# Layer 0's opening: first product without the identity, loads reordered, band patterns stored in the order read, first band read unguarded

## The chip, the core and the metric

The kernel runs on one core of a Trainium2 chip. A core has five engines that run their own instruction streams: PE (matrix products and transposes, with weight loads as a stream of their own), DVE and ACT (elementwise work and reductions), POOL (elementwise, slower) and SP, which here only issues DMAs. ACT also issues some. DMAs run on 16 DMA engines; an engine issues one and goes on, and whoever needs the data waits on a semaphore. The metric is the device time of one execution in microseconds, the median of several.

## What is computed

A four-layer network on tensors of 8 x 512 tokens x 128 channels. The change lies at the start of layer 0, an attention with 16 heads of 8 channels and relative positions in logarithmic buckets (DeBERTa's form). Before it the tokens are normalised (NT = 32 tiles of 128 tokens). Cut to what matters:

```python
q = split_heads(hidden_states @ Wq + bq)
k = split_heads(hidden_states @ Wk + bk)
v = split_heads(hidden_states @ Wv + bv)
scores = jnp.einsum('bhqd,bhkd->bhqk', q, k) / scale
rel = build_relative_position(S, S, BUCKETS, MAX_REL)
pos_k = (rel_embeddings @ Wk + bk).reshape(2 * ATT_SPAN, nH, d)
c2p_att = jnp.einsum('bhqd,hpd->bhqp', q, pos_k)
c2p = jnp.take_along_axis(c2p_att, c2p_pos, axis=-1)
p2c_att = jnp.einsum('bhkd,hpd->bhkp', k, pos_k)
p2c = jnp.swapaxes(jnp.take_along_axis(p2c_att, p2c_pos, axis=-1), -1, -2)
scores = scores + (c2p + p2c) / scale
probs = jax.nn.softmax(scores, axis=-1)
```

## The kernel before

Every engine has its own function per layer (`l0_pe`, `l0_dv`, `l0_ac`, `l0_po`, `l0_sp`); the order of the work on an engine is the order in which that function writes it, and semaphores join them. `Engine.wait_ge` leaves out a wait already seen.

**Setup.** `run_sp` and `run_ac` issue the first loads: `relT`, `oh`, `pat` (SP) and `wk`, `bkt` (ACT) count on `ld_pos`, five times 16 = 80; `X[:, 0:8]` (512 KB) on `ld_end`, the rest of x (1536 KB) on `ld_x`, the identity on `ld_id`, the other small ones on `ld[0]`. PE multiplies `relT` by `wk` (the position keys), DVE adds `bkt` (`posk`), PE multiplies `posk` by `oh`: these are the band patterns PGF. DVE and ACT split PGF into three 16-bit parts, `PGS` (128 x 3 x 256). SP writes PGS to DRAM (`pgd`) and reads it back in another layout into `PGO`, whose 16 matrices of 128 x 128 for each of two sides hold, for one head each, 8 rows at the places that `PLACES` lists. Meanwhile DVE normalises the tokens in four groups of 8 tiles (`norm_stats`, `root`, `tokens`) into `XN`, PE transposes them, four tiles at a time (eight times, `n_tr`), and ACT copies them to `XT` (`n_xt`). `root(c)` on DVE waits for a square root by ACT (`norm_root`), which stands behind patterns and copies in ACT's order.

**Split q and k.** PE makes q and k of the first sequence, ACT and DVE split them in 16-bit parts (`split_ac`, `split`). SP writes these parts to DRAM (`q_write(0, 0)`, `q_write(0, 1)`: three DMAs each, `q_write(0, 2)`: one) and loads them again by groups of four heads (`load_group`, `load_upper`).

**Bands.** For head n, `g_of(n, 0)` and `g_of(n, 1)` on PE multiply these by `PGO`, DVE's `g_out` adds a step that POOL made (`corr`) and puts the sums into `GG[n % 2]`, which must have been cleared once. SP writes GG to DRAM (`write(n)`) and reads it back one element shorter per row (`read(n)`), which shifts each row by its number, into `CD[n % 3]`. CD[0] lies in the arena AR; CD[1] and CD[2] lie in XN's memory, and so may only be written once all XN tiles have been transposed: `read` waits for `n_tr` 8. POOL masks a band (`own_band`), PE adds its transpose to the scores, DVE adds the masked own part (`add`), takes the maximum (`most`), ACT exponentiates.

**Loop.** 128 heads x 4 steps (`STEPS0` = 512 + 28). In each step PE does at most one small product of the next sequence, one `g_of`, the transposes of an earlier step, and the scores. `G_AT`, `CORR_AT`, `WRITE_AT` and `READ_AT` say at which step what is issued.

Of the kernel before, what the change touches and what calls it, by code (L numbers as in the profile page):

```python
# [12 lines left out]
NB, NT, NH = 8, 32, 16  # L13
# [129 lines left out]
def flat(ap):  # L143
    return ap.rearrange("p a b -> p (a b)")
# [83 lines left out]
def program(nc, a, out):  # L228
    ctx = ExitStack()
    with ctx:  # L230
# [6 lines left out]
        X = sb("X", [128, NT, 128])  # L237
# [180 lines left out]

        PT_0, XN_0, GG_0 = 1, 2, 5
        PGO_0, VA_0, HALF_0 = 1, 3, 4  # L420
        sgn, set_mm, set_dv, set_ac, sel_ok, pg_w, pg_r = (sem("set_" + k) for k in ("sgn", "mm", "dv", "ac", "sel", "pgw", "pgr"))
# [55 lines left out]
        def l0_pe(pe):  # L477
            pe.wait_ge(ld_id, 16)
            pe.wait_ge(ld_pos, 80)
# [109 lines left out]
            def pv(G, jb):  # L589
# [10 lines left out]
                if jb == 3:  # L600
                    ins.then_inc(pv_mm, 1)

            pe.wait_ge(dv_init, XN_0)
            for j in range(4):
# [12 lines left out]
            pe.wait_ge(*emptied[number["g0", 0, 0]])  # L617
            pe.wait_ge(pg_r, 12 * 16)
            pe.wait_ge(dv_init, GG_0)
            for n in range(2):  # L620
# [22 lines left out]
        def l0_dv(dv):  # L643
# [68 lines left out]
            tokens(12, 16).then_inc(n_xd, 1)  # L712
            for k in range(2):
                dv.e.memset(GG[k], 0.0).then_inc(dv_init, 1)
            norm_stats(dv, 0, NT0, 2, False)
# [11 lines left out]
            def g_out(n, x):  # L727

                dv.wait_ge(g_mm, 2 * n + x + 1)
                dv.wait_ge(p_cr, 2 * n + x + 1)  # L730
                dv.wait_ge(dv_init, GG_0)
                if n >= 2:
# [215 lines left out]
        def l0_po(po):  # L948
            po.e.memset(PGO, 0.0).then_inc(po_init, 1)
            for k in range(2):  # L950
                po.e.memset(VA[k], 1.0).then_inc(po_init, 1)
            po.e.memset(minus_half, -0.5).then_inc(po_init, 1)
# [68 lines left out]
        def l0_sp(sp):  # L1021
            sp.wait_ge(set_dv, 6)
            sp.wait_ge(set_ac, 2)
            sp.e.dma_start(pgd, PGS).then_inc(pg_w, 16)
            sp.wait_ge(pg_w, 16)
            sp.wait_ge(po_init, PGO_0)
            for k in range(2):
                for part, first, step, times in PLACES[1 - k]:
                    for x in range(first, first + step * times, step):
                        src = bass.AP(pgd.tensor, part * 256 + k * 128, [[16 * 768, 8], [768, 16], [1, 128]])  # L1030
                        sp.e.dma_start(PGO[8 * x:8 * x + 8, k], src).then_inc(pg_r, 16)

# [49 lines left out]
            def read(n):  # L1082

                sp.wait_ge(wr[n % 2], 16 * (n // 2 + 1))
                sp.wait_ge(n_tr, 8)
                if n >= 3:
                    sp.wait_ge(s_mm, 4 * (n - 2))
                    sp.wait_ge(p_w, 2 * (n - 2))
                src = bass.AP(scr.tensor, n % SLOTS * 128 * ROW + 64, [[ROW - 1, 128], [1, BACK]])
                sp.e.dma_start(CD[n % 3], src).then_inc(rd[n % 3], 16)  # L1090
# [1660 lines left out]
        def run_ac(g):  # L2751
# [3 lines left out]
            ac.e.dma_start(X[:, 0:8, :], a["x"][:, 0:8, :]).then_inc(ld_end, 16)  # L2755
            ac.e.dma_start(X[:, 8:NT, :], a["x"][:, 8:NT, :]).then_inc(ld_x, 16)
            ac.e.dma_start(wo, a["l0_wo"]).then_inc(ld[0], 16)
# [31 lines left out]
        def run_sp(g):  # L2789
            sp = Engine(g, own["sp"])  # L2790
            for dst, name in ((relT, "relT"), (oh, "oh"), (pat, "pat")):
                sp.e.dma_start(dst, a[name]).then_inc(ld_pos, 16)
            sp.e.dma_start(ident192[:, :], a["ident"]).then_inc(ld_id, 16)
            for dst, name in ((wq, "l0_wq"), (colb, "l0_cols"), (mask16, "mask16"), (wv, "l0_wv"), (bvt, "l0_bvt"),
                              (steps, "steps"), (window, "window"), (sw, "l0_sw")):
                sp.e.dma_start(dst, a[name]).then_inc(ld[0], 16)
            l0_sp(sp)
            after_l0(sp)
# [85 lines left out]
```

## Time and profile before

| | |
|---|---|
| Median of 3 executions | 2166.33 us (2162.15 to 2167.49) |
| The profiled execution | 2157.39 us, span 2155.6 us |
| Mean granted clock of PE | 0.966 of full speed |
| Busy: PE, DVE, ACT, POOL | 89%, 79%, 67%, 56% of the span |
| DMA | 264.01 MB, 122 GB/s in the mean, 263 to 312 GB/s in slices 2 to 16 of 40 |

The profile is one execution. The span runs from its first to its last instruction; 1.8 us lie around it. A row of the timeline gives the start and length of an instruction, or of several merged ones (xN), and in brackets how long the engine had been idle before it and what ended that. Layer 0 takes about the first 890 us of the span.

### The profile page before, as it was taken

Reading aid. Unit: us, or ns where it says so; the run is one execution under the profiler, and the core shown is the slowest. Engines: PE = TensorE matmul, PEld = TensorE weight load, DVE = VectorE, ACT = ScalarE, POOL = GpSimd, SP = SyncE. Lnnn points to the kernel's source line nnn. Section 1 sums busy time; section 2 is a strip of 40 time slices with the busy share of each in tenths; the row PEclk is TensorE's granted clock in tenths of the full one; section 3 lists DMA queues with packets and bytes.
Section 4 is the critical chain, followed back from the end, with each engine's and each line's share of the span. In section 5 each row is a group of like instructions: output and inputs, shape, how many; then the busy total and the mean of one; then the engine's idle time right before and its main releaser. Section 6 shows DMA issues by size and latency. Waiting matters only on the chain.

```text
span 2155.6 us, 38856 instructions
## 1 busy us (share of the span) xinstructions
PE 1913.3 (89%) x13526; PEld 1457.8 (68%) x13526; DVE 1694.2 (79%) x3929; ACT 1453.9 (67%) x2882; POOL 1210.8 (56%) x1024
## 2 busy tenths in 40 slices
PE   3799899999999998688987899999999978889998
PEld 2566666666666666455575688888887756668797
DVE  6688989898889898657358788888888877774686
ACT  5678687777777777543423767777777777776675
POOL 2778787778777777336434355555555544437300
PEclk8899999999999999869998999999999999999999
DMA  4898788888888887210100000000001000002000
GB/s 150 295 312 303 269 305 277 297 284 294 281 296 280 300 282 263 92 58 1 39 1 6 1 1 1 1 1 1 1 1 31 1 1 1 1 16 89 25 1 40
DMA packets 73107, 264.01 MB, mean 122 GB/s; under 512 B 11632, under 2 KB 31344, under 8 KB 72400
## 3 DMA queue, kind: packets, MB, share of 16 engines
q1 hardware_dynamic: 71968, 255.06, 35.0%
q10 hardware_dynamic: 944, 6.46, 0.8%
q8 instruction: 109, 1.79, 0.3%
q14 instruction: 86, 0.70, 0.1%
HBM read 140.17 MB, written 121.31 MB: 121 GB/s over the span
## 4 chain that ended last, share of the span: by engine, by line
PE 40%; ACT 6%; DVE 6%; issue 1%; POOL 1%; DVEq 0%; ACTq 0%; POOLq 0%
PE PS L157 10%; PE PS L335 8%; PE PS L161 8%; PE PS L163 7%; PE PS L162 7%; ACT AR L167 3%; ACT L167 1%; DVE DR L181 1%; DVE AR L185 1%; ACT PT L171 1%; DVE PT L181 1%; POOL AR L176 1%; DVE AR L181 1%; ACT AR L171 0%; DVE AR L193 0%
## 5 line engine op out<-in xcount | busy, mean ns | idle before, releaser
L167 ACT ACTIVATE AR<-PS,AR 128x512 f32<-128x512 f32 x1024 | 699.0, 690 | 276.8 <-DVE AR L193 179.0
L193 DVE TENSOR_REDUCE AR<-PS 128x1 f32<-128x512 f32 x896 | 614.6, 686 | 91.6 <-PE PS L163 76.1
L335 PE MATMUL PS<-ident,AR 128*128 128x128 f32 x3816 | 583.8, 277 | 54.0 <-ACT AR L171 18.7
L157 PE MATMUL PS<-AR 128*9 128x512 f32 (+8 forms) x4190 | 495.0, 357 | 98.9 <-DVE AR L181 41.2
L335 PEld LDWEIGHTS PS<-ident,AR 128*128 128x128 f32 x3816 | 432.0, 142 | 168.1 <-issue 54.1
L181 POOL TENSOR_TENSOR AR<-AR 128x512 f32<-128x512 f32 (+6 forms) x325 | 389.6, 1215 | 233.1 <-DVE AR L181 113.6
L157 PEld LDWEIGHTS PS<-AR 128*9 128x9 f32 (+5 forms) x4190 | 286.2, 132 | 304.0 <-DVE AR L181 135.5
L176 POOL TENSOR_SCALAR AR<-AR 128x512 f32<-128x512 f32 (+1 forms) x146 | 251.7, 1724 | 274.1 <-DVE AR L1727 204.5
L171 ACT ACTIVATE AR<-PS 128x512 f32<-128x512 f32 (+3 forms) x596 | 347.7, 588 | 82.0 <-PE PS L335 48.0
L171 ACT ACTIVATE PT<-PS 128x512 fp32r<-128x512 f32 x320 | 191.5, 598 | 165.7 <-PE PS L335 131.8
L181 DVE TENSOR_TENSOR PS<-PS,AR 128x192 f32<-128x192 f32 (+1 forms) x512 | 201.3, 393 | 103.1 <-PE PS L578 92.8
L181 DVE TENSOR_TENSOR AR<-PS,AR 128x512 f32<-128x512 f32 (+3 forms) x321 | 209.6, 654 | 38.7 <-PE PS L157 36.6
L181 POOL TENSOR_TENSOR AR<-XN,AR 128x192 f32<-128x192 f32 (+1 forms) x170 | 201.7, 1208 | 39.5 <-DMA XN<-scr 29.1
L181 DVE TENSOR_TENSOR PT<-PS,PT 128x512 fp32r<-128x512 f32 x320 | 217.0, 679 | 8.6 <-ACT PT L171 8.6
L578 PE MATMUL PS<-AR 128*128 128x320 bf16 (+3 forms) x1024 | 196.1, 273 | 0.0
L181 POOL TENSOR_TENSOR AR<-AR,XN 128x512 f32<-128x512 f32 x144 | 154.4, 1074 | 72.0 <-DVE AR L181 69.2
L575 PE MATMUL PS<-ident,XN 128*128 128x128 f32 x680 | 130.3, 273 | 0.0
L161 PE MATMUL PS<-MH,XNr 128*128 128x512 f32 x256 | 122.7, 479 | 5.3 <-ACT AR L167 2.9
L578 PEld LDWEIGHTS PS<-AR 128*128 128x128 bf16 x1024 | 100.5, 98 | 6.0
L161 PE MATMUL PS<-PT,VW 128*128 128x512 f32 x256 | 102.0, 399 | 0.0
L163 PE MATMUL PS<-MH,XNr 128*128 128x512 f32 x256 | 101.9, 398 | 0.0
L162 PE MATMUL PS<-MH,XL 128*128 128x512 f32 x256 | 101.4, 396 | 0.0
(173 smaller groups left out, 2942.3 us busy)
## 6 DMA issues: line engine op xcount, KB each, us to landing
scr<-AR SPq DMA_DIRECT2D x128, 800.0 KB, 4.2
XN<-scr SPq DMA_DIRECT2D x85, 768.0 KB, 6.6
AR<-scr SPq DMA_DIRECT2D x43, 768.0 KB, 6.4
AR<-qsc SPq DMA_DIRECT2D x96, 192.0 KB
qsc<-AR SPq DMA_DIRECT2D x16, 384.0 KB, 4.5
qsc<-AR SPq DMA_DIRECT2D x16, 256.0 KB, 4.5
AR<-in_wgu SPq DMA_DIRECT2D x16, 256.0 KB, 3.0
qsc<-AR SPq DMA_DIRECT2D x16, 128.0 KB, 5.0
```

The lines of the kernel that those rows point to most:

```text
L157: return pe.e.matmul(out, lhsT, rhs, start=start, stop=stop)
L161: pe.e.matmul(out, l[0], r[0], start=start, stop=False)
L162: pe.e.matmul(out, l[1], r[0], start=False, stop=False)
L163: return pe.e.matmul(out, l[0], r[1], start=False, stop=stop)
L167: return ac.e.activation(out, in_, func, bias=bias, scale=scale, accum_out=accum)
L171: return ac.e.activation(out, in_, ACT.Copy, bias=0.0, scale=1.0)
L176: return en.e.tensor_scalar(out, in0, s1, None, op0)
L181: return en.e.tensor_tensor(out, in0, in1, op)
L193: return dv.e.tensor_reduce(out, in_, AX.X, ALU.max, negate=True)
L335: return pe.e.transpose(out, in_, ident[0:k, 0:k])
L575: pe.e.matmul(out, lhsT, rhs, start=start, stop=start, is_transpose=True, skip_group_check=True)
L578: return pe.e.matmul(out, lhsT, rhs, start=False, stop=stop, skip_group_check=True)
```

## The change

- PE's first product no longer waits for the identity (`ld_id`); that wait stands before the first transposes, which use it.
- The identity's load goes from SP's queue to ACT's, behind `X[:, 0:8]`. The rest of x goes from ACT's queue to the end of SP's first loads.
- The patterns lie in DRAM by part and side, 2048 elements (4 KB) for each group of 8 rows, in the order in which PGO takes them. The write is one DMA of 128 x 6 runs of 256 B; the reads are eight DMAs instead of twelve, and a read of three neighbouring places repeats its source.
- The two clears of GG go from DVE to POOL, and the waits for them follow (`po_init` for `dv_init`).
- `read(n)` waits for `n_tr` 8 only where n is no multiple of 3.

```diff
@@ l0_pe
-            pe.wait_ge(ld_id, 16)
             pe.wait_ge(ld_pos, 80)
             mm(pe, PS[0:64, 7, 0:128], relT, wk, True, True).then_inc(set_mm, 1)
...
+            pe.wait_ge(ld_id, 16)
             pe.wait_ge(dv_init, XN_0)
...
-            pe.wait_ge(pg_r, 12 * 16)
-            pe.wait_ge(dv_init, GG_0)
+            pe.wait_ge(pg_r, 8 * 16)
+            pe.wait_ge(dv_init, PV_0)
@@ l0_dv
-            for k in range(2):
-                dv.e.memset(GG[k], 0.0).then_inc(dv_init, 1)
             norm_stats(dv, 0, NT0, 2, False)
...
-                dv.wait_ge(dv_init, GG_0)
+                dv.wait_ge(po_init, GG_0)
@@ l0_po
             po.e.memset(PGO, 0.0).then_inc(po_init, 1)
             for k in range(2):
+                po.e.memset(GG[k], 0.0).then_inc(po_init, 1)
+            for k in range(2):
                 po.e.memset(VA[k], 1.0).then_inc(po_init, 1)
@@ l0_sp
-            sp.e.dma_start(pgd, PGS).then_inc(pg_w, 16)
+            sp.e.dma_start(bass.AP(pgd.tensor, 0, [[128, 128], [128 * 128, 6], [1, 128]]),
+                           flat(PGS).rearrange("p (a s) -> p a s", a=6)).then_inc(pg_w, 16)
             sp.wait_ge(pg_w, 16)
             sp.wait_ge(po_init, PGO_0)
             for k in range(2):
                 for part, first, step, times in PLACES[1 - k]:
-                    for x in range(first, first + step * times, step):
-                        src = bass.AP(pgd.tensor, part * 256 + k * 128, [[16 * 768, 8], [768, 16], [1, 128]])
-                        sp.e.dma_start(PGO[8 * x:8 * x + 8, k], src).then_inc(pg_r, 16)
+                    for x in range(first, first + step * times, step if step > 1 else times):
+                        n = times if step == 1 else 1
+                        src = bass.AP(pgd.tensor, (2 * part + k) * 128 * 128, [[0, n], [2048, 8], [1, 2048]])
+                        sp.e.dma_start(flat(PGO[8 * x:8 * (x + n), k]), src).then_inc(pg_r, 16)
@@ read
-                sp.wait_ge(n_tr, 8)
+                if n % 3:
+                    sp.wait_ge(n_tr, 8)
@@ run_ac
-            ac.e.dma_start(X[:, 8:NT, :], a["x"][:, 8:NT, :]).then_inc(ld_x, 16)
+            ac.e.dma_start(ident192[:, :], a["ident"]).then_inc(ld_id, 16)
@@ run_sp
-            sp.e.dma_start(ident192[:, :], a["ident"]).then_inc(ld_id, 16)
             for dst, name in ((wq, "l0_wq"), (colb, "l0_cols"), (mask16, "mask16"), (wv, "l0_wv"), (bvt, "l0_bvt"),
                               (steps, "steps"), (window, "window"), (sw, "l0_sw")):
                 sp.e.dma_start(dst, a[name]).then_inc(ld[0], 16)
+            sp.e.dma_start(X[:, 8:NT, :], a["x"][:, 8:NT, :]).then_inc(ld_x, 16)
```

PE at the start of the program, before and then after the change; `ld_pos` and `ld_id` are the counts of the position loads and of the identity's load:

```order
L157 MATMUL PS<-AR 64x128 [waits ld_pos,ld_id]
L157 MATMUL PS<-AR 128x256 [waits set_dv]
L157 MATMUL PS<-AR 128x2
L335 MATMUL PS<-ident,XN 128x128 [waits dv_init]
L335 MATMUL PS<-ident,XN 128x128 x3
```

```order
L157 MATMUL PS<-AR 64x128 [waits ld_pos]
L157 MATMUL PS<-AR 128x256 [waits set_dv]
L157 MATMUL PS<-AR 128x2
L335 MATMUL PS<-ident,XN 128x128 [waits dv_init,ld_id]
L335 MATMUL PS<-ident,XN 128x128 x3
```

The wait for the identity has moved from the first row to the first transpose; the instructions are the same.

SP's queue from its last small load to the last write of split q and k, before and then after:

```order
L2796 DMA AR<-in_l_sw 128x128
L1024 DMA pgd<-AR 128x768 [waits set_ac,set_dv]
L1031 DMA AR<-pgd 8x16x128 [waits po_init,set_pgw]
L1031 DMA AR<-pgd 8x16x128 x11
L1048 DMA qsc<-AR 128x3x512 [waits l0_sp_a,l0_sp_p]
L1048 DMA qsc<-AR 128x2x512
L1048 DMA qsc<-AR 128x512
L1048 DMA qsc<-AR 128x3x512 [waits l0_sp_a,l0_sp_p]
L1048 DMA qsc<-AR 128x2x512
L1048 DMA qsc<-AR 128x512
L1043 DMA qsc<-AR 64x1536 [waits l0_sp_a,l0_sp_p]
```

```order
L2798 DMA AR<-in_l_sw 128x128
L2799 DMA X<-in_x 128x3072
L1024 DMA pgd<-AR 128x6x128 [waits set_ac,set_dv]
L1033 DMA AR<-pgd 24x1x2048 [waits po_init,set_pgw]
L1033 DMA AR<-pgd 8x2048 x3
L1033 DMA AR<-pgd 24x1x2048
L1033 DMA AR<-pgd 8x2048 x3
L1050 DMA qsc<-AR 128x3x512 [waits l0_sp_a,l0_sp_p]
L1050 DMA qsc<-AR 128x2x512
L1050 DMA qsc<-AR 128x512
L1050 DMA qsc<-AR 128x3x512 [waits l0_sp_a,l0_sp_p]
```

The rest of x is one more DMA ahead of the patterns' write, and eight reads with long rows stand where twelve with short ones stood, ahead of the same writes.

SP around the first two band reads (`AR<-scr` is read(0), `XN<-scr` is read(1)), before and then after:

```order
L1080 DMA scr<-AR 128x1600 [waits l0_g_o] x2
L1090 DMA AR<-scr 128x1536 [waits n_tr,l0_wr0]
L1090 DMA XN<-scr 128x1536 [waits l0_wr1]
L1102 DMA XN<-in_l_lnsc 128x128
L1102 DMA XN<-in_l_lnb 128x128
```

```order
L1082 DMA scr<-AR 128x1600 [waits l0_g_o] x2
L1093 DMA AR<-scr 128x1536 [waits l0_wr0]
L1093 DMA XN<-scr 128x1536 [waits n_tr,l0_wr1]
L1105 DMA XN<-in_l_lnsc 128x128
L1105 DMA XN<-in_l_lnb 128x128
```

The wait for the transposes (`n_tr`) has moved from the first read to the second.

## Rows read from the trace of the kernel before

**Rows 1.** Timeline, first 20 us: start, length, engine, line, operation, [idle before <-what ended it].

```profile
7.42 0.43 SPq L2796 DMA_DIRECT2D AR<-in_l_sw  x1
7.44 2.00 ACT L167 ACTIVATE AR<-AR 128x2048 bf16<-128x2048 f32 x1 [2.60 <-DMA AR<-in_pat]
...
11.56 0.69 PE L157 MATMUL PS<-AR 128*64 128x128 f32 x2 [11.56 <-DMA ident<-in_ident]
...
17.74 1.12 PE L335 MATMUL PS<-ident,XN 128*128 128x128 f32 x4 [3.60 <-DVE XN L177]
...
19.61 1.58 DVE L200 BATCH_NORM_STATS2 AR<-X 128x6 f32<-128x128 f32 x8
```

**Rows 2.** DMA issues of the first 100 us: size, median us from issue to landing.

```profile
scr<-AR SPq DMA_DIRECT2D x9, 800.0 KB, 5.2
...
X<-in_x ACTq DMA_DIRECT2D x1, 1536.0 KB, 8.9
...
pgd<-AR SPq DMA_DIRECT2D x1, 192.0 KB, 2.2
qsc<-AR SPq DMA_DIRECT2D x1, 192.0 KB, 2.9
```

**Rows 3.** Timeline of SP's DMA issues, 18 to 55 us.

```profile
19.07 0.33 SPq L1024 DMA_DIRECT2D pgd<-AR  x1
21.34 8.44 SPq L1031 DMA_DIRECT2D AR<-pgd  x12
29.88 3.88 SPq L1048 DMA_DIRECT2D qsc<-AR  x6
33.86 0.64 SPq L1043 DMA_DIRECT2D qsc<-AR  x1
36.79 0.34 SPq L1063 DMA_DIRECT2D AR<-qsc  x1
...
43.70 2.88 SPq L1080 DMA_DIRECT2D scr<-AR  x2
54.33 0.32 SPq L1090 DMA_DIRECT2D AR<-scr  x1
```

**Rows 4.** Timeline, DVE, 24 to 43 us.

```profile
24.81 2.08 DVE L181 TENSOR_TENSOR AR<-AR 128x512 f32<-128x512 f32 x3 [0.77 <-ACT AR L171]
...
30.95 0.67 DVE L181 TENSOR_TENSOR AR<-AR 64x512 bf16<-64x512 f32 x1
...
32.94 1.39 DVE L714 MEMSET AR<- 128x1600 f32 x1 [0.28 <-issue]
...
38.72 0.20 DVE L208 RECIPROCAL AR<-AR 128x8 f32<-128x8 f32 x1 [0.34 <-ACT AR L167]
...
42.38 1.29 DVE L181 TENSOR_TENSOR AR<-PS,AR 128x512 f32<-128x512 f32 x2 [0.47 <-PE PS L157]
```

**Rows 5.** Timeline, ACT, 35 to 39 us.

```profile
35.20 1.99 ACT L167 ACTIVATE AR<-AR 128x2048 bf16<-128x2048 f32 x1
```

**Rows 6.** Timeline, start of the loop over heads: PE, POOL and DVE.

```profile
54.94 0.61 PE L157 MATMUL PS<-AR 128*128 128x128 bf16 x4 [0.69 <-ACT XT L171]
...
58.59 4.54 POOL L181 TENSOR_TENSOR AR<-AR 128x192 f32<-128x192 f32 x4 [11.85 <-DMA AR<-scr]
...
58.66 0.66 PE L575 MATMUL PS<-ident,AR 128*128 128x128 f32 x2 [3.11 <-DMA AR<-scr]
...
59.54 1.92 PE L157 MATMUL PS<-XT,AR 128*128 128x512 f32 x2
61.05 0.37 DVE L181 TENSOR_TENSOR PS<-PS,AR 128x192 f32<-128x192 f32 x1 [8.29 <-POOL AR L181]
...
62.06 0.40 PE L157 MATMUL PS<-AR 128*128 128x128 bf16 x4 [0.60 <-DVE AR L181]
```

**Rows 7.** Windows of the loop: us, busy (x instructions) by engine, TensorE clock, DMA share, GB/s.

```profile
107.00:155.00 48.00, 45.76 (x411) 32.52 (x412) 42.98 (x87) 38.09 (x69) 36.95 (x34) 1.00 0.92 317
```

**Rows 8.** Line 578, both score products of a step: count, duration, first and last start.

```profile
L578 PE MATMUL PS<-AR x1024: 192/299/562, 59.1 to 887.1; 128*128 128x64 bf16 x43, 128*128 128x448 bf16 x43, 128*128 128x320 bf16 x43, 128*128 128x192 bf16 x42
```

## What the change will do: prediction

> **What bounds the kernel now.** The change touches only the opening of layer 0, so the busy shares over the whole span say little: PE, DVE and DMA are all occupied in the loop over heads (DMA at 0.92 of its engines in a typical window, [rows 7]), and nothing there is edited. I read the timeline of the first 62 us engine by engine, asking at every gap what ended it. Four places decide when the loop starts.
>
> First, PE's first product starts at 11.56, released by the landing of the identity [rows 1], although its operands had all landed by 7.44: ACT's first pattern, which waits for the same count of position loads, starts there [rows 1]. Everything on DVE and ACT hangs on this product.
>
> Second, SP's queue. It writes the band patterns at 19.07, then spends 21.34 to 29.78 issuing twelve reads of them, then 29.88 to 33.76 issuing six writes of the split q and k, then the seventh at 33.86 [rows 3]. The first head group's load can only be issued at 36.79 [rows 3], and DVE's first band sum comes at 42.38 [rows 4].
>
> Third, DVE between 32.94 and 42.38: two clears of 1.39 us (one row of the two is shown), statistics, a root that waits for ACT, and a normalisation that ends at 42.38 - 0.47 = 41.91 [rows 4]. It has only 0.47 us of slack against the band product.
>
> Fourth, the first read of a band from DRAM, at 54.33 [rows 3]. It waits for the last transposes of XN, although its target is not in XN. PE is through its last preparation product at 54.94 + 0.61 = 55.55, idles 3.11 us until this read lands at 58.6, and DVE's first sum into the scores starts at 61.05, after POOL has masked the band [rows 6].
>
> **Part by part.**
>
> *First product without the identity.* It goes from 11.56 to 7.44: 4.1 us earlier. What it needs and shared the queues with (position loads, the first 512 KB of x) keeps its place. The identity now has 0.5 MB ahead of it instead of 2 MB; it is next needed by the transposes, 17.74 - 4.1 = 13.6 [rows 1], and landed at 11.56 even in its old place, so it costs nothing. Bounds: 3.1 (the pattern load a microsecond later) to 5.1 (a microsecond earlier).
>
> *Loads in another order.* The rest of x, 1536 KB, leaves ACT's queue and is now SP's last load. SP issued its last small load at 7.42 [rows 1]; with the identity gone from SP the x load takes about that place. It landed 8.9 us after issue when it shared the engines with everything else [rows 2], so at the latest at 16.4. DVE reaches the statistics that need it at 19.61 - 4.1 = 15.5 [rows 1]. With most other loads ahead of it and nothing behind, I take it as landed by then: 0, at most 0.9 lost.
>
> *Band patterns in the order read.* The write of 192 KB becomes 768 pieces of 256 B instead of 128 of 1536 B; the twelve reads (128 pieces each) become eight with rows of 4 KB, two of 24 rows, six of 8. The write goes out at 19.07 - 4.1 = 15.0. It landed in 2.2 us in large pieces, a write to DRAM of the same size in 2.9 [rows 2]; for six times the pieces I take 3.5 and allow twice the 2.9, 5.8. A read cost SP 8.44 / 12 = 0.70 us; a load with 4 KB rows costs 0.34 and a gap of a few hundredths [rows 3]. So eight cost 3.0 (5.6 at the old rate). SP is free for q and k at 15.0 + 3.5 + 3.0 = 21.5. q's parts are ready after the second of DVE's three splits at 24.81, about 26.2 [rows 4], now 22.1. So here the reads leave the path and DVE's splits take their place. The six writes take 4.0 [rows 3], to 26.1. The seventh needs DVE's last split, 30.95 + 0.67 [rows 4], now 27.5. It thus goes at 27.5 instead of 33.86, and the group's load at 36.79 - 6.3 = 30.5. SP has 1.4 us to spare. At the far ends (5.8 and 5.6) the seventh goes at 15.0 + 5.8 + 5.6 + 4.0 = 30.4, 2.9 us later.
>
> *The clears go from DVE to POOL.* POOL's next work follows DVE's first scales, which come just before the transposes (now 13.6); two clears after its others hide there even at twice DVE's 1.39 each. DVE loses 3.3 us of work. But its root needs ACT, and ACT's pattern, 35.20 to 37.19 [rows 5], moves only by 4.1, to 33.1. So the step of DVE at 38.72 [rows 4] goes to 33.4, not to 31.3, and the normalisation ends 3.2 later, at 36.6. The load chain would allow the band sum at 42.38 - 6.3 = 36.1. The later of the two counts: 36.65, which is **5.7 us earlier** than 42.38. Had the clears stayed, it would be 4.1 + 0.5.
>
> *First band's read unguarded.* All up to the last preparation product keeps its spacing: it ends at 55.55 - 5.7 = 49.8. The first band's write goes at 43.70 - 5.7 = 38.0, the second's at 40.5 (the pair takes 2.88 [rows 3]). The write lands 2.9 to 5.2 after its issue (the lower as the 192 KB write, the upper the median of its own kind [rows 2]), so the read goes between 40.9 and 43.2; it takes 4.3 (54.33 to 58.6 [rows 3, 6]), or 2.5 more if the second write's 800 KB stand ahead at 317 GB/s [rows 7]. It lands between 45.2 and 50.0. The 3.1 us wait of PE is gone, and POOL's mask (58.59 to 61.05, 2.46) mostly runs beside the end of the preparation. DVE's first sum then waits for the score products themselves, 49.8 + 1.1 = 50.9, against 61.05: 10.1 us earlier. Far end: 50.0 + 2.5 = 52.5, 1.6 worse. PE then still has the q product of the next sequence, 0.88 after the score product's start and 1.92 long [rows 6]: 49.8 + 0.88 + 1.92 = 52.6, where the next band product started at 62.06. So **9.5 us earlier** in all. Had the read kept its guard, 5.7 would be the whole. The second band's read keeps the guard, is issued near 48.6 and lands 4.3 to 6.8 later, by 55.4; the second head starts four steps of 1.62 after 50.9, at 57.4.
>
> *The loop itself.* 512 steps take 59.1 to 887.1 [rows 8], 1.62 us each. All that feeds it is issued relative to its own steps, so I take its length as unchanged.
>
> *A page's rule on the reads.* The new reads of 24 rows start with a repeat of 3. Rows of before show no transfer of that shape. The Trainium skill, DMA: Bandwidth & Descriptors, section "Why a DMA increments its semaphore by 16 and not by 1", says that a DMA uses the largest number of engines up to 16 that divides the slowest dimension on both sides, which is 3 here; no row of before can confirm it. It is weighed as a rival below.
>
> **Sum.** 4.1 (first product), 1.6 more by SP's queue and the clears, 3.8 net by the first read: 9.5. The profiled execution took 2157.4 (span 2155.6), 8.9 under the median 2166.3 of the three unprofiled runs, which lie 5.3 apart. The sum is a shift of what comes after, so it is taken off either: 2147.9 for a profiled execution, and 2166.3 - 9.5 = **2156.8** for the median.
>
> **Rivals.**
>
> *Given back in the loop.* DMA is at 0.92 of its engines from 107 on [rows 7]. If the early heads are limited by transfers rather than by PE and DVE, the head start counts only as far as the first band write moved, 5.7: 2160.6. For: that share. Against: the gap before 62.06 names DVE, not a transfer [rows 6], and the transfers move with the steps.
>
> *The first product is not freed.* If another load of the same count arrives late, the 4.1 is lost and 9.5 - 4.1 = 5.4 stays: 2160.9. Against it stands ACT's start at 7.44 [rows 1].
>
> *SP's queue late.* With the far ends of write and reads the seventh write goes 2.9 later, of which 0.5 is covered by DVE: 9.5 - 2.4 = 7.1, 2159.2.
>
> *Reads on few engines.* Two reads of 24 rows would put 8 x 4 KB x 2 = 66 KB on each of three engines. At 317 / 0.92 / 16 = 21.5 GB/s per engine [rows 7] that is 3.0 us, done by 23, before the q writes matter. At half that rate it is 6.1, plus 2.3 for the six small reads: from 18.5 to 26.9, then these engines' share of the q and k writes, 96 KB or 4.5 us, and the end, some 2.6, at 34.0 instead of 30.5. That leaves 9.5 - 3.0 = 6.5: 2159.8. That is what the page's rule, cited above, could cost.
>
> *Slower.* The loop's pace is set by how write, read and masking of a band interlock over 128 heads. If the new start puts band reads just behind the step that needs them, and each step takes 2% longer, that is 828 x 0.02 = 16.6 us: 2173.4. It turns the sign from 9.5 / 828 = 1.15% on. No row before shows a pace that depends on the start.
>
> **Numbers.** Forecast case (2153 to 2159) 0.61; given back 0.18; first product not freed 0.06; SP late 0.06; few engines 0.03; slower 0.06. About 0.3%, 6.5 us, is what a measurement of this kernel tells from no change, so faster means under 2159.8: 0.61 + 0.06 = 0.67. Same: 0.18 + 0.06 + 0.03 = 0.27. Slower: 0.06. The range goes from 2150.5 (the upper bound 5.1 at the start, and the spread of the runs below) to 2164.5 (the rivals at 2161 with the spread above).
>
> **What would show it.** In the trace after: PE's first product near 7.4; SP's pattern write near 15.0, reads taking 3 us, the seventh write near 27.5, the group load near 30.5; DVE's first band sum near 36.7; the first read issued by 43 and no wait of PE for it; first sum into the scores near 50.9; last step of the loop near 877.5. A pattern write over 5 us, a statistics step of DVE that waits for x past 15.5, or a loop longer than 830 us would make it wrong.

## The result, and the profile after

| | before | after |
|---|---|---|
| Median of 4 executions each, run side by side | 2164.48 us (2162.15 to 2167.49) | 2149.68 us (2146.59 to 2153.20) |
| Ratio | | 0.9931, interval 0.9908 to 0.9955 |
| The profiled execution | 2157.39 us, span 2155.6 | 2151.93 us, span 2150.1 |
| Mean granted clock of PE in it | 0.966 | 0.964 |

The kernel became 14.8 us faster by the medians. The forecast was 2156.8 with a range from 2150.5 to 2164.5: the sign held, the time lies 0.8 us below the range. The two profiled executions differ by only 5.5 us, and that gap between 14.8 and 5.5 is the main subject of what follows.

First the opening. The timeline of the kernel after in its first 20 us (start, length, engine, line, operation, idle before and what ended it), to be read against [rows 1]:

```profile
6.23 2.00 ACT L167 ACTIVATE AR<-AR 128x2048 bf16<-128x2048 f32 x1 [1.40 <-DMA AR<-in_pat]
6.25 0.69 PE L157 MATMUL PS<-AR 128*64 128x128 f32 x2 [6.25 <-DMA AR<-in_pat]
6.45 0.43 SPq L2799 DMA_DIRECT2D X<-in_x  x1
12.51 1.09 PE L335 MATMUL PS<-ident,XN 128*128 128x128 f32 x4 [3.68 <-DVE XN L177]
14.29 1.61 DVE L200 BATCH_NORM_STATS2 AR<-X 128x6 f32<-128x128 f32 x8
```

PE's first product and ACT's first pattern are now released by the same load, `pat`, which itself landed 1.2 us earlier than before. The product moved by 5.3 us, not 4.1. The statistics that need the rest of x start at 14.29 without a wait: reordering the loads cost nothing.

SP's queue of the kernel after, 12 to 56 us, against [rows 3]:

```profile
13.76 0.39 SPq L1024 DMA_DIRECT2D pgd<-AR  x1
16.07 3.88 SPq L1033 DMA_DIRECT2D AR<-pgd  x8
20.89 4.13 SPq L1050 DMA_DIRECT2D qsc<-AR  x6
26.49 0.51 SPq L1045 DMA_DIRECT2D qsc<-AR  x1
29.11 0.33 SPq L1065 DMA_DIRECT2D AR<-qsc  x1
...
36.65 2.91 SPq L1082 DMA_DIRECT2D scr<-AR  x2
39.99 0.32 SPq L1093 DMA_DIRECT2D AR<-scr  x1
47.33 0.32 SPq L1093 DMA_DIRECT2D XN<-scr  x1
```

The patterns' write in 256 B pieces let its first read go 2.3 us after its issue, as the write in large pieces had. The eight reads took 3.88 us of SP, 0.48 each. The head group's load goes at 29.11, 7.7 us earlier, and the first bands' write at 36.65, 7.1 us earlier than 43.70 [rows 3]. The first read follows at 39.99; the second keeps the guard and goes at 47.33.

DVE, PE and POOL of the same kernel, from single rows of their timelines between 27 and 52 us, against [rows 4, 6]:

```profile
27.55 1.97 PE L325 MATMUL PS<-ident,XN 128*128 128x128 f32 x8 [4.39 <-DVE XN L177]
32.23 0.20 DVE L208 RECIPROCAL AR<-AR 128x8 f32<-128x8 f32 x1 [2.31 <-ACT AR L167]
34.20 1.01 PE L157 MATMUL PS<-AR 128*128 128x128 bf16 x8 [4.69 <-DMA AR<-qsc]
35.34 1.28 DVE L181 TENSOR_TENSOR AR<-PS,AR 128x512 f32<-128x512 f32 x2
45.31 1.94 PE L325 MATMUL PS<-ident,XN 128*128 128x128 f32 x8 [7.01 <-DVE XN L177]
45.65 3.36 POOL L181 TENSOR_TENSOR AR<-AR 128x192 f32<-128x192 f32 x3 [5.92 <-DMA AR<-scr]
48.77 0.64 PE L577 MATMUL PS<-AR 128*128 128x64 bf16 x2
49.44 0.37 DVE L181 TENSOR_TENSOR PS<-PS,AR 128x192 f32<-128x192 f32 x1 [3.67 <-PE PS L577]
50.91 0.63 PE L157 MATMUL PS<-AR 128*128 128x128 bf16 x4
```

DVE's root waits 2.31 us for ACT: what the moved clears freed stops there, as the prediction said. POOL masks the first band from 45.65, before PE comes to the scores, and DVE's first sum into them waits for the products themselves. The next head's band product starts at 50.91 against 62.06 [rows 6], 11.15 us earlier.

That lead is not kept. Windows of both kernels (columns: stretch, its length, busy and count of PE, PEld, DVE, ACT, POOL, granted clock of PE, DMA share, GB/s), first of the kernel before, then of the one after:

```profile
27.00:57.50 30.50, 8.93 (x54) 7.58 (x53) 22.13 (x81) 16.81 (x19) 5.26 (x5) 0.62 0.60 175
57.50:95.00 37.50, 27.24 (x210) 20.32 (x211) 25.14 (x48) 21.68 (x39) 29.78 (x28) 0.90 0.84 285
```

```profile
27.00:57.50 30.50, 16.18 (x75) 11.42 (x76) 19.14 (x76) 15.72 (x19) 11.90 (x11) 0.50 0.63 187
57.50:95.00 37.50, 29.14 (x246) 21.99 (x244) 27.40 (x53) 25.71 (x47) 30.53 (x28) 0.95 0.95 324
```

At 0.50 of full speed, the lower of PE's two levels (1.2 GHz), PE of the kernel after worked through its last preparation and its first steps of the loop, after it had idled 4.4 us ahead of 27.55, 4.7 us ahead of 34.20 and 7.0 us ahead of 45.31. In windows of 1 us and less the kernel after is at half clock up to 57.3, which takes in 8.5 us of its loop; the kernel before is at half clock up to 61.6, which takes in only the first 2.5 us of its own. So part of the head start was run at half speed. The time at half clock itself is not longer: up to the write of band 9 it is 34.1 us in each of two profiles of the kernel after and 30.7 to 37.5 us (mean 33.6) in seven of the kernel before. In the kernel before more of it falls where PE waits. The write of band 9 shows what was left, 102.99 before and 94.62 after, 8.4 us:

```profile
102.99 0.34 SPq L1080 DMA_DIRECT2D scr<-AR  x1
```

```profile
94.62 0.35 SPq L1082 DMA_DIRECT2D scr<-AR  x1
```

The loop ends with this line, against [rows 8]; its last step starts 6.8 us earlier than 887.1, where 877.5 was expected:

```profile
L577 PE MATMUL PS<-AR x1024: 192/299/581, 48.8 to 880.3; 128*128 128x64 bf16 x43, 128*128 128x448 bf16 x43, 128*128 128x320 bf16 x43, 128*128 128x192 bf16 x42
```

### The profile page after: what moved, and what is told of

It is laid out like the page before. It is cut to its first block, busy times and chain, and to the rows that moved or that the text cites. A ratio compares the mean times of both kernels' runs of the same rounds, so it can differ in the third digit from the quotient of the medians.

```text
span 2150.1 us, 38852 instructions
## 1 busy us (share of the span) xinstructions
PE 1919.4 (89%) x13526; PEld 1463.6 (68%) x13526; DVE 1690.3 (79%) x3927; ACT 1453.9 (68%) x2882; POOL 1216.0 (57%) x1026
## 4 chain that ended last, share of the span: by engine, by line
PE 41%; ACT 6%; DVE 6%; POOL 1%; issue 1%; DVEq 0%; ACTq 0%; POOLq 0%
PE PS L157 11%; PE PS L335 8%; PE PS L161 8%; PE PS L163 7%; PE PS L162 7%; ACT AR L167 3%; ACT L167 1%; DVE DR L181 1%; DVE AR L185 1%; ACT PT L171 1%; DVE PT L181 1%; POOL AR L176 1%; DVE AR L193 1%; POOL X L181 0%; DVE AR L181 0%
```

## The experiments

Two measures are used throughout. Medians are set against executions of the kernel before on the same chip. Beside them stands a time at equal clock, an estimate: over 93 executions of the kernel before (2156.8 to 2170.2 us, mean 2162.9) the time falls by 1.06 us for each 0.001 of mean granted clock, with 1.7 us left over, and this line is used to bring each execution to 0.966. The kernel before comes to 2159.2 there. Twice the standard error of such a time is 0.7 to 1.5 us for the kernels below without added products, and 2.3 for the clears. In the traces three legs are compared: up to SP's write of band 9, from there to the write of band 127, and the rest of the span, which is the later layers.

In these figures band 9 is the tenth band, counted from 0; it is the write at 94.62 that some expectations call the eighth head's.

**Both kernels again.** No edit. 

> The changed kernel, unaltered, timed again beside the kernel before. Theory S (the gain is the shift at the opening, carried on unchanged): the trace after has the 4th to 8th step of the loop 9.1 us earlier and the rest 8.3 to 8.5 earlier until a single interruption near 542 us, so 8 to 10 us less, ratio about 0.996. Theory L (the loop or later layers became quicker too): 13 to 16 us less, ratio about 0.993.

> The kernel before, unaltered, profiled a second time. Theory P (its first trace, at 2157.4, was one of its quick executions; the usual one has PE at half its clock through the first heads): an execution near 2164 whose granted clock is at half over most of 32 to 80 us, with the 8th head's write later than 103.0 by up to 5 us, the rest in single low windows inside the loop. Theory L (the loop's own length differs between the kernels): 8th head's write at 103.0 as in the first trace, and the loop from there on 5 us longer at the same clock.

> The same, a third time; same numbers by each theory. Three traces of the kernel before show where its executions differ.

> The kernel before, one more profiled execution. Theory P (an execution that is slow because TensorE stays at half clock through the first heads): if its mean granted clock is 0.960 or less, the extra half-clock time lies between 30 and 85 us, unbroken, and the eighth head is later than the 103 us of the first profile. Rival W: the extra half-clock time is single falls later in the head loop or in the later layers. With a mean of 0.963 or more it says nothing.

> The kernel before, another profiled execution. Theory P: if its mean granted clock is 0.960 or less, the extra half-clock time lies between 30 and 85 us, unbroken. Rival W: single falls later in the program. With a mean of 0.963 or more it says nothing.

> The kernel before, a third profiled execution of this set. Theory P: if its mean granted clock is 0.960 or less, the extra half-clock time lies between 30 and 85 us, unbroken. Rival W: single falls later in the program. With a mean of 0.963 or more it says nothing.

> The kernel before, one more profiled execution. Theory P: if its mean granted clock is 0.960 or less, the extra half-clock time lies between 30 and 85 us, unbroken. Rival W: single falls later in the program. With a mean of 0.963 or more it says nothing.

The kernel after again: 2148.51 (2147.27 to 2150.84), ratio 0.9932, interval 0.9918 to 0.9945. Nine executions of it have a mean of 2149.4 and a mean clock of 0.9657; at equal clock 2149.1. The six profiled executions of the kernel before took 2161.8, 2159.7, 2161.7, 2161.0, 2161.3 and 2163.7, at clocks from 0.963 to 0.967. The legs, in us:

| profiles | to band 9 | to band 127 | rest | span |
|---|---|---|---|---|
| before, mean of 7 (range) | 103.7 (102.7 to 104.6) | 763.9 (762.2 to 766.1) | 1291.6 (1289.9 to 1293.5) | 2159.1 |
| after, mean of 2 | 94.5 | 764.0 | 1289.8 | 2148.4 |
| difference | 9.2 | -0.1 | 1.8 | 10.7 |

The shift of the opening is 9.2 us and the loop keeps it. By its time the pair came out as theory L had said (15.3 us by the medians, ratio 0.9932), but not by L's cause: the loop is no quicker, and the 1.8 us in the later layers are less than the 3.6 us by which the two profiles after differ there (1291.7 and 1288.0). The shift itself is what theory S had said. The first profile of the kernel before, on which the forecast was built, was the quickest of the seven in the loop and near the quickest of all executions in time. The two profiles taken to tell one long stay at half clock from a longer loop show neither: band 9 at 102.7 and 104.6, and a loop leg 3.1 and 1.1 us longer than in the first, where theory L had 5. None of the seven has a mean clock of 0.960 or less, as 24 of the 93 executions have, so the question for which the last four were run stays open for the kernel before.

**First product and loads alone**, on the kernel before:

```diff
@@ l0_pe
-            pe.wait_ge(ld_id, 16)
             pe.wait_ge(ld_pos, 80)
...
+            pe.wait_ge(ld_id, 16)
             pe.wait_ge(dv_init, XN_0)
@@ run_ac, run_sp: identity to ACT's queue, rest of x to the end of SP's first loads
```

> The kernel before with the loads in the new order and the first product freed of the identity; the patterns' layout, the clears and the guarded read stay. Theory S: first product at 6.25 as in the trace after, 5.3 earlier, and since SP's queue follows the pattern write all of it is passed on: group load at 31.5, first band sum near 37.1, last transposes near 49, total 5.3 less. Theory Q (SP's queue or the clears on DVE hold it up): 2 to 3 less.

> The kernel of p_first once more (clock 0.956 and 58.0 us unbroken at half clock from 24.3 in its first profile; other executions of it had up to 0.966). Theory P: with a mean granted clock of 0.963 or more the half-clock time of the opening is broken before 82 us, and the lead over before at the eighth head is near its first 5 us, not near 0. Rival W: the stay is unbroken again and the mean is made up elsewhere.

2158.06, ratio 0.9977 (0.9964 to 0.9990); at equal clock 2154.8, 4.4 under the kernel before. The first bands' write goes at 37.97, 5.7 us earlier, by this edit alone. Then the two profiled executions of this one kernel part. The first took 2161.78 at a mean clock of 0.956, the second 2152.18 at 0.966. PE's row of the second head's first scores, first execution and second:

```profile
57.27 0.63 PE L577 MATMUL PS<-AR 128*128 128x192 bf16 x2
```

```profile
57.44 0.38 PE L577 MATMUL PS<-AR 128*128 128x192 bf16 x2
```

Windows of the first, then of the second:

```profile
24.50:57.00 32.50, 11.43 (x55) 8.45 (x56) 20.59 (x78) 14.31 (x15) 7.14 (x8) 0.50 0.63 194
58.00:82.00 24.00, 17.50 (x86) 13.05 (x87) 12.49 (x24) 9.15 (x16) 15.25 (x15) 0.50 0.72 235
...
900.00:2150.00 1250.00, 1132.88 (x6746) 903.77 (x6746) 934.37 (x2244) 791.03 (x1712) 561.92 (x433) 0.95 0.04 13
```

```profile
24.50:57.00 32.50, 11.16 (x53) 8.17 (x54) 21.01 (x77) 14.99 (x16) 8.05 (x9) 0.58 0.64 194
58.00:82.00 24.00, 17.08 (x120) 13.19 (x122) 16.19 (x32) 13.21 (x23) 18.73 (x18) 0.79 0.83 278
...
900.00:2150.00 1250.00, 1126.28 (x6740) 896.77 (x6738) 931.41 (x2246) 790.89 (x1712) 564.71 (x433) 0.96 0.05 15
```

The same instructions reached the same place within 0.2 us of each other, and one execution stayed at half clock for 24 us more and did 86 products in them, where the other did 120. The second was at full clock from 57.4 only to about 67, then at half for another 10 us. The write of band 9 came at 103.00 in the first, 0.7 us earlier than the mean of 103.7 before: nearly all of the 5.7 us had been given back. In the second it came at 99.11. That is 3.9 of the 9.6 us between them; the loop gives -0.7 and the later layers 6.4. Theory P had a lead near 5 for the second and got 4.6 against the mean of 103.7; it had not said that most of the difference lies in the later layers. The Trainium skill, TensorE: Matmul & The Clock Gate, section "What's actually happening", says that the number of slow products at the start of one kernel differs from run to run, and puts the price of that ramp under 1% of a typical span. These two agree, though their stay is not at the kernel's start: the 9.6 us between them are 0.4% of the span, the 3.9 us of the opening 0.2%, and yet those are four tenths of this change's shift.

**Patterns' layout alone**, on the kernel before: the edits of `pgd`'s write and reads and the wait for 8 reads in place of 12.

> The kernel before with the patterns' new layout in DRAM alone (one write in 256 B pieces, eight reads). Theory S: pattern write at 19.1, reads done by 25.4, the seventh write of split q and k at DVE's last split, 31.7, group load at 34.6 (2.2 earlier), but DVE's normalisation with the clears still ends at 41.9, so the first band sum gains 0.4 and the total 0.5, not to be told from no change. Theory Q (SP's queue is the path by itself): 2.2 to 4 less.

2161.80, ratio 0.9994 (0.9984 to 1.0003), at equal clock 0.1 less than before. Rows of its SP, DVE and PE timelines:

```profile
31.92 0.51 SPq L1045 DMA_DIRECT2D qsc<-AR  x1
34.53 0.33 SPq L1065 DMA_DIRECT2D AR<-qsc  x1
38.99 0.20 DVE L208 RECIPROCAL AR<-AR 128x8 f32<-128x8 f32 x1 [0.34 <-ACT AR L167]
39.97 1.01 PE L157 MATMUL PS<-AR 128*128 128x128 bf16 x8 [5.03 <-DMA AR<-qsc]
43.41 2.91 SPq L1082 DMA_DIRECT2D scr<-AR  x2
```

The group's load goes 2.3 us and the band product 1.8 us earlier than before. The bands' write moves by only 0.3, less than the 0.7 us by which it differs among the seven profiles before (43.47 to 44.13), because DVE comes to its root at 38.99, 0.3 later than in [rows 4], with the clears still ahead of it.

**The first read alone**, on the kernel before, and the change without it:

```diff
@@ read, on the kernel before
-                sp.wait_ge(n_tr, 8)
+                if n % 3:
+                    sp.wait_ge(n_tr, 8)
@@ read, on the kernel after
-                if n % 3:
-                    sp.wait_ge(n_tr, 8)
+                sp.wait_ge(n_tr, 8)
```

> The kernel before with the first band's read unguarded alone. Theory S: read at about 47.1 instead of 54.3, no wait of PE for it at 58.66, first sum into the scores near 56.6 instead of 61.05, total 2 (if PE then does the first head at half its clock, as in the trace after) to 4 less. Theory N (the second band's read, still guarded, takes its place): under 1 less.

> The changed kernel with the guard put back on the first band's read. The prediction's own term: 3.8 us more than the changed kernel (first sum into the scores near 53.9 instead of 49.4). With the clock: 2 to 6 more, since it adds an idle stretch of 3 us to PE just before the loop.

Alone: 2158.95, ratio 0.9978 (0.9967 to 0.9989); at equal clock 3.0 under the kernel before, inside the 2 to 4 of theory S. The read goes at 47.21 and the first sum follows at 56.63, both as expected; band 9 is written at 99.05, 4.6 us before the mean of 103.7:

```profile
56.63 0.37 DVE L181 TENSOR_TENSOR PS<-PS,AR 128x192 f32<-128x192 f32 x1 [3.68 <-PE PS L578]
```

Taken out of the change: 2156.48, ratio to the kernel before 0.9969 (0.9957 to 0.9981); the change without it is 8.0 us slower by the medians and 3.5 at equal clock. DVE's first sum and a window of the change without it:

```profile
53.94 0.37 DVE L181 TENSOR_TENSOR PS<-PS,AR 128x192 f32<-128x192 f32 x1 [8.31 <-POOL AR L181]
```

```profile
57.50:80.50 23.00, 17.50 (x86) 13.06 (x87) 11.48 (x22) 8.86 (x15) 14.24 (x14) 0.50 0.75 244
```

The sum comes 4.5 us later than 49.44, near the price of the wait. Then PE stayed at half clock up to 80.5, and band 9 was written at 101.84, 7.2 later than with the read freed. So removing PE's 3 us wait paid twice in these executions: by the wait, and by the way the clock came back. The second part rests on single profiles and differs between executions, as the pair above shows. But the clocks of all executions bear it out. The two profiles with a mean clock of 0.960 or less are the first of the first product alone and this one, with 58.0 and 54.6 us at half clock up to band 9; every other profile without added products has at most 41.0. Of the four kernels in which the first read is guarded, 33 of 130 executions have such a clock (24 of 93, 4 of 13, 1 of 12, 4 of 12). Of the four in which it is free (the kernel after, the read alone, and the two experiments that follow) none of 39 has. Why the wait of 3 us lets the stay grow is not shown.

**Clears back on DVE**, on the kernel after:

```diff
             tokens(12, 16).then_inc(n_xd, 1)
+            for k in range(2):
+                dv.e.memset(GG[k], 0.0).then_inc(dv_init, 1)
@@ l0_po
-            for k in range(2):
-                po.e.memset(GG[k], 0.0).then_inc(po_init, 1)
```

> The changed kernel with the two clears back on DVE. Prediction's term: first band sum near 36.4 instead of 35.3, so 1.1 us more in all. If clears on POOL hinder nothing and DVE were free anyway: 0.

2150.45, ratio to before 0.9950 (0.9932 to 0.9968); at equal clock 1.2 above the change, which seven executions do not tell from nothing (twice the standard error of the difference is 2.4). The trace carries it: the bands' write goes at 37.84 in place of 36.65, 1.2 later, and band 9 at 95.35, 0.8 later than the mean of 94.5. Here its profile took 2158.27, with 768.2 us for the loop leg, in which PE fell to half clock five times.

**A delay put into the opening**, on the kernel after, ahead of the position keys' sum on DVE:

```diff
             dv.e.memset(zero, 0.0).then_inc(dv_init, 1)
+            for _ in range(5):
+                dv.step(dv.e.memset(XNf[:, 1024:3072], 0.0))
+                dv.settle()
```

> The changed kernel with a delay of about 4.8 us put in the opening's VectorE row (five more clears of stored tiles ahead of the first statistics). Theory S (the opening's shift is carried one to one to the end): 4.8 us more than the changed kernel at equal clock, and the eighth head's write 4.8 us later than 94.6. Theory P: what is beyond that comes with the mean granted clock, at 1.05 us for each 0.001. Rival: at equal clock more than 8 or less than 2.

The delay was mis-sized: PE's second product moved from 7.39 to 14.53, and the bands' write by 7.1, from 36.65:

```profile
14.53 1.44 PE L157 MATMUL PS<-AR 64*128 64x256 f32 x4 [7.48 <-DVE AR L181]
```

```profile
43.70 2.91 SPq L1085 DMA_DIRECT2D scr<-AR  x2
```

Band 9 was written at 101.76, 7.2 after the mean of the change's two profiles. The time was 2158.82 (0.9984, 0.9973 to 0.9996, against before), at equal clock 2156.5: 7.4 above the change, with 1.4 as twice the standard error (9.1 by the means as they are, because the clock differs too). Within that a shift of the opening is carried to the end one to one, from the trace and from twelve executions.

**PE's idle stretches filled**, on both kernels and in two sizes, with products of zeros into a bank that the next use clears:

```diff
+            def keep_busy(n):
+                z = zero.bitcast(BF)
+                for _ in range(n):
+                    pe.e.matmul(PS[:, B_PV, :], z[:, 0:128], z[:, 0:512], start=True, stop=True)
...
+            keep_busy(15)
             norm_tr(pe, 0, 2, 4, 2)
             norm_tr(pe, 0, 3, 4, 3)
+            keep_busy(18)
...
                 g_of(n, 1)
+                if n:
+                    keep_busy(27)
```

> The changed kernel with 15, 18 and 27 such products in the same three gaps. Theory P: PE at full clock through the first heads; 2 to 3 us less than the changed kernel (in its trace the lead falls from 11.1 to 9.1 us while PE runs the first head at half its clock), and 9 to 11 us less than the kernel before with its gaps filled, which is the pure shift of the opening. Theory L: same as the changed kernel, 14 to 15 less than the kernel before with its gaps filled.

> The kernel before, with 17, 28 and 28 products of zeros (128x128 by 128x512, 16-bit, into a bank that holds zeros) put into PE's three long gaps of the opening, so that its granted clock doesn't fall there; the layers' work is unchanged. Theory P (part of the change's gain is time that PE otherwise spends at half its clock over the loop's first heads, more or less of it from execution to execution): clock at 1.00 from 30 to 80 us, 4 to 7 us less in the median than the kernel before, and a narrower spread of the runs than its 11 us. Theory L (the clock at the opening doesn't matter, the loop is faster for another reason): same time within 1 us, same spread.

> The kernel before with 17, 36 and 30 products of zeros in PE's gaps of the opening and 12 more before the first score product, where PE waits for the first band; the first filled version had left 3.4 us idle there and its clock had fallen twice. Theory P: clock at 1.00 at the start of the loop, 4 to 7 us less than the kernel before, spread under 5 us. Theory L: within 1 us of the kernel before.

On the kernel after: 2142.52 (2142.23 to 2144.46), ratio to before 0.9908 (0.9890 to 0.9926), 6.0 us under the median of 2148.51 and the fastest kernel of this study; none of the nine executions of the kernel after, at least 2146.59, comes near. That is twice what theory P had for it, and the 19.4 us to the first filled kernel before fit neither theory's figure. On the kernel before, with 17, 28 and 28: 2161.89, ratio 0.9992 (0.9979 to 1.0005), nothing. With 17, 36, 30 and 12 more ahead of the first scores: 2157.21 (2155.89 to 2162.19), ratio 0.9973 (0.9961 to 0.9985), 5.9 us under the median of 2163.07 on its chip, as much as theory P gave. Windows, first of the filled kernel after, then of the first filled kernel before:

```profile
27.00:57.50 30.50, 20.81 (x139) 12.05 (x140) 22.61 (x83) 17.51 (x22) 13.30 (x13) 1.00 0.71 213
```

```profile
27.00:57.50 30.50, 24.98 (x135) 14.33 (x133) 22.59 (x83) 16.85 (x20) 5.26 (x5) 0.89 0.56 158
57.50:95.00 37.50, 25.87 (x198) 19.31 (x199) 23.65 (x46) 20.53 (x37) 29.65 (x28) 0.91 0.84 293
```

The same 30.5 us ran at 0.50 in the change and at 1.00 with the gaps filled, and band 9 was written at 89.75, 4.7 earlier than 94.5. In the kernel before the first filling raised the clock of the stretch before 57.5 only, where its PE had little to do but wait, and left the first heads near where they were (0.91, where the seven profiles have 0.79 to 0.90). There is also a cost that was not foreseen: its bands' write went at 45.98, 2.3 later than 43.70 [rows 3]. The group's load had gone 1.8 later; 0.4 of it stands in the first product already (11.98 against 11.56), the rest is open. Theory P's amount came in the second filling, but its mechanism did not: the window from 27 to 57.5 is at 0.96 and the next at 0.85, and band 9 goes 2.3 us later than the mean of 103.7 all the same.

```profile
106.02 0.34 SPq L1092 DMA_DIRECT2D scr<-AR  x1
```

So up to band 9 full clock paid in the kernel after, where PE's own work set the pace, and not in the kernel before, where PE waited. What the second filling gains lies behind band 9. For the filled kernels the time at equal clock means little, since filler at full clock raises the mean without shortening anything. In the filled kernel after, 4.2 us of the loop leg are gone too (759.8 against 764.0), as in the second filled kernel before (759.8, under all seven profiles before) but not in the first (763.6); that is not explained, and so only the 4.7 us up to band 9 are shown as the price of half clock.

**Two more reorderings on top**: ACT's roots ahead of its patterns, DVE's fourth statistics ahead of the band sums, gaps filled with 15, 18 and 20.

```diff
             norm_xt1(ac, 0, 3, 3)
-            pattern(OP[1][1], 1)
             norm_root(ac, 0, NT0, 2)
+            pattern(OP[1][1], 1)
...
+            norm_stats(dv, 0, NT0, 3, False)
             for n in range(2):
                 g_out(n, 0)
                 g_out(n, 1)
-            norm_stats(dv, 0, NT0, 3, False)
             root(3)
```

> The changed kernel with filled gaps (15, 18 and 20 products), and two reorderings: ACT's square root of the third group of tokens ahead of a pattern, and DVE's statistics of the fourth group (with ACT's root) ahead of the band sums. Expected by the rows of the trace after: DVE's third root at 29.8 instead of 32.2, last transposes 2 to 2.5 us earlier, so 2 us less than the filled version, near 2140.5. By the rival (the transfers of the first bands then decide): same as the filled version, 2142.5.

2145.94 (2142.57 to 2149.78), ratio 0.9912 (0.9896 to 0.9929): not faster than filling alone. DVE's first sum, here and then in the filled kernel after:

```profile
48.27 0.37 DVE L181 TENSOR_TENSOR PS<-PS,AR 128x192 f32<-128x192 f32 x1 [4.82 <-POOL AR L181]
```

```profile
47.54 0.37 DVE L181 TENSOR_TENSOR PS<-PS,AR 128x192 f32<-128x192 f32 x1 [2.23 <-PE PS L577]
```

PE's last transposes had started 1.9 us earlier (43.00 against 44.86), but the sum now waited for POOL's mask and so for the first band's read. That read had gained nothing: with the statistics ahead of the band sums it went 0.8 us later (40.79 against 40.01). The bound of the first sum had passed from PE to the transfer. That explains 0.7 of the 2.6 us by which band 9 came later (92.37 against 89.75). The rest goes with a second difference, which this experiment does not separate: with 20 products in the last gap in place of 27, PE was at half clock for 13.6 us up to band 9, against 3.4.

## Why the prediction was wrong

The steps that failed are the base, a median of three executions taken as firm, and the gain taken as a pure shift with no term for PE's clock. Taking the steps in order:

- *First product.* 5.3 us where 4.1 was taken and 5.1 was the upper bound. The cause was right; `pat` landed 1.2 us sooner, more than the microsecond allowed.
- *Loads.* Nothing lost, as forecast.
- *Patterns.* The write was over-priced, 2.3 us against 3.5, and the reads under-priced, 3.9 against 3.0; together 6.2 against 6.5. The 0.34 us came from loads with another form of row. That DVE's splits take the place of the reads held: SP waited from 19.95 to 20.89 before the q writes.
- *Clears and root.* The mechanism held exactly: DVE waits 2.31 us for ACT. The band sum went 7.0 us earlier, not 5.7; 1.2 of the 1.3 more is the first product's. Clears on DVE cost 1.2 in the trace, where 1.1 follows from the prediction's 5.7 against 4.6.
- *First read.* That the guard cost PE a wait of about 3 us held: with it put back, the first sum came 4.5 us later. Issued at 39.99, just ahead of the 40.9 to 43.2 given. The first sum came at 49.44 against 50.9, the next band product at 50.91 against 52.6: 11.15 us of lead, not 9.5. Of the 1.65 more, 1.2 is the first product's again.
- *The lead is kept.* This step failed in kind. PE at half its clock ran the first 8.5 us of the loop, where in the kernel before it did so for 2.5, and 11.15 us became 9.2 by band 9. The prediction had no term for the clock. The two errors nearly cancelled, which was luck: 9.2 us at band 9 in the traces, and 10.1 at equal clock, against 9.5.
- *The loop.* Unchanged in the mean, 763.9 and 764.0 us. The rival in which the gain is given back to the transfers falls, though DMA rose to 0.95 of its engines in the first heads. So does the rival of a pace upset by the new start and, since the group's load went at 29.11 and not at 34.0, the reads on few engines. By the Trainium skill, DMA: Bandwidth & Descriptors, section "Why a DMA increments its semaphore by 16 and not by 1", the two reads of 24 rows would have used three engines; the trace does not say which they used, and no wait shows a price.

So the shift was right within a microsecond, by errors that cancelled, and the forecast still lay 7.1 us too high. Two steps did that.

First, **the base**. 2166.3 was the median of three executions. Over the 87 executions that stood beside the second timing of the changed kernel and the experiments, the median of the kernel before is 2162.9, so the base stood 3.4 us too high. The prediction saw the spread of 5.3 us and that the profiled execution lay 8.9 lower, and took the median of three as firm.

Second, **the gain as a pure shift**. The means of all executions lie 13.5 us apart (2162.9 and 2149.4). Of these 10.1 are left at equal clock. The other 3.4 go with the mean clock, 0.9626 before and 0.9657 after. The prediction had no step by which a change in the opening alters how long PE is at half clock, and so neither the gain nor the range had room for it. The profiles show no shorter stay at half clock in the opening (34.1 us after, 33.6 in the mean before). What the runs do show is that the executions with a mean clock of 0.960 or less are gone: 24 of 93 before, none of nine after, and none of 39 in all kernels whose first read is free. Without those 24 the mean of the kernel before is 1.4 us lower, 2161.5 at a clock of 0.9639. So about 1.4 of the 3.4 us go with the first read's guard; this is an estimate, for no profile caught such an execution of the kernel before. Where the other 2 us lie is open.

The parts do not add up either, which the prediction's chain had right. At equal clock the first product alone gives 4.4, the read 3.0, the layout 0.1: 7.5 of 10.1. The remaining 2.6 (twice the standard error is about 2.3) would be what clears and layout give together, each freeing nothing while the other still stands in the way. For the layout that is shown: alone, it stops at DVE's clears. For the clears it is argued, since they were never moved alone, and the layout was never taken out of the change.

## What to carry to other kernels

Cost the idle time of PE in an opening by what PE does next, too: products that follow a gap at half clock run at half speed, and a head start can be spent on them; filling the gaps with idle products gave 6 us here, of which 4.7 lay where PE-bound work followed. Where waits followed it gained nothing there; one of the two fillings still made the whole 5.9 us shorter, behind band 9, which is not explained. A shift is carried one to one through a steady loop, but measure it from many executions: a base of three and one profile left 3.4 and 5.5 us of error here, as large as some of the parts. Where two edits each feed the same join, expect little from one of them alone (the layout alone gave 0.1 us), and take each out of the whole before judging it.

## What was not expected of the hardware

- One kernel, with PE at the same work at 57.3 us in two executions, was at half clock to 82 us in one; in the other it was at full clock from 57.4 to 67 and then at half for 10 us. The first wrote band 9 3.9 us later.
- Executions at a mean clock of 0.960 or less were 33 of 130 where PE waited 3 us for the first band's read, and none of 39 where it did not.
- The kernel before spreads over 13.4 us (2156.8 to 2170.2); with the kernel after's gaps filled, five executions lie within 2.2.
- Writing 192 KB to DRAM took 2.3 us as 768 pieces of 256 B in the changed kernel and 2.2 as 128 of 1536 B. Over the other kernels the same write took 2.3 to 3.1 us in small pieces (3.0 in the layout alone) and 1.8 to 2.3 in large ones, so a price of up to 1.3 us is not excluded.
- SP's cost of issuing a read followed its form: 0.70 us for 128 short pieces [rows 3], 0.48 for 8 or 24 rows of 4 KB.
